# Holding back three of four gather groups on GpSimd until VectorE has made scores 0, 2 and the logits

## The reference

```python
# layer 0: deformable attention over 9 sampled points per pixel, 8 groups of 32 channels
qkv = depthwise3x3(groupnorm(x) @ qkv_w + qkv_b)
for g in range(8):
    off  = pconv_einsum(q, off_pconv_w[g], off_w[g]) + base[g]          # 9 (x, y) per pixel
    k, v = warp(k_map[g], off) * mask, warp(v_map[g], off) * mask       # bilinear, 4 corners
attn = softmax(q . k)                                                   # over the 9 points
x = x + (attn . v) @ proj_w + proj_b
# layer 1: attention of 8 heads over all 4096 tokens of an image, with 3-tap convolutions
t = layernorm(x); q, k, v = conv3(t), conv3(t), conv3(t)
t = x + t + conv3(softmax(q k^T / sqrt(32)) v)
# then a mixture of 8 experts (256 -> 1024 -> 256), each token sent to its best one
t = t + moe(layernorm(t))
```

## Time and profile before

| what | value |
|---|---|
| median of the runs | 12329.67 us |
| the profiled execution, its span | 12255.1 us |
| mean granted TensorE clock | 0.81 of 2.4 GHz |
| TensorE matmuls busy | 8279.2 us, 68% |
| VectorE busy | 5175.9 us, 42% |
| ScalarE busy | 3780.5 us, 31% |
| GpSimd busy | 4967.5 us, 41% |
| gathers of the sampling, L661 | 4608, of 1022 ns each on average |

### The profile page before, as it was taken

The page is one execution under the profiler, slowest core; times in us unless marked ns, Lnnn a source line. Parts: engine busy times, 40 slices in busy tenths (PEclk is TensorE's granted clock), DMA queues, the critical chain, the costliest instruction groups (busy, mean ns, idle before and its releaser), DMA issues. The chain is left out here.

```text
span 12255.1 us, 95913 instructions
## 1 busy us (share of the span) xinstructions
PE 8279.2 (68%) x31522; PEld 4334.5 (35%) x31522; DVE 5175.9 (42%) x10029; ACT 3780.5 (31%) x5495; POOL 4967.5 (41%) x4864
## 2 busy tenths in 40 slices
PE   6544656445663576666667765666666888998699
PEld 3522323332332233332333332333333333443366
DVE  6522334344443454444434443444444435663333
ACT  2100003001441144332434442324324563553122
POOL 1255564555445454454445554544554200000222
PEclk9776877666886688886878887778878898999799
DMA  3833233555332433333332334333343212113321
GB/s 133 281 93 89 92 124 111 185 194 158 95 91 86 128 99 97 93 100 107 94 97 89 103 91 121 110 114 99 98 123 95 70 45 74 41 45 80 123 71 49
DMA packets 658541, 1283.55 MB, mean 105 GB/s; under 512 B 189043, under 2 KB 398218, under 8 KB 643408
## 3 DMA queue, kind: packets, MB, share of 16 engines
q0 software_dynamic: 234240, 639.57, 17.4%
q1 hardware_dynamic: 405392, 562.58, 15.4%
q10 hardware_dynamic: 18432, 75.51, 1.5%
HBM read 1003.44 MB, written 278.91 MB: 105 GB/s over the span
## 5 line engine op out<-in xcount | busy, mean ns | idle before, releaser
L661 POOL DMA_INDIRECT sa_slot<-s_table,sa_rec x4608 | 4710.2, 1022 | 4902.7 <-DVE sa_vals L759 2347.2
L1651 DVE CUSTOM_DVE_ANT_0 a_above<-a_late,a_above 128x512 f32<-128x512 f32 x1600 | 1103.8, 690 | 3209.4 <-remote 1358.3
L1592 ACT ACTIVATE a_above<-a_diff 128x512 f32<-128x512 f32 x1600 | 956.4, 598 | 3189.2 <-DMA s_kd<-p_diff_lo 1408.5
L1558 PE MATMUL a_ctx<-a_p,a_v 128*64 128x512 f32 x6400 | 1714.9, 660 | 95.3 <-issue 95.2
L1583 ACT ACTIVATE a_p<-a_s 128x1024 f32<-128x1024 f32 x1600 | 1628.7, 1020 | 322.4 <-remote 163.3
L1503 PE MATMUL a_late<-a_k,a_q 96*128 96x512 f32 x1600 | 859.6, 537 | 838.5 <-DVE a_pair_max L1651 446.0
L1491 PE MATMUL a_diff<-a_kd,a_q 96*128 96x512 f32 x1600 | 773.9, 484 | 848.1 <-issue 460.6
L1541 PE MATMUL a_s<-a_q,a_k 98*128 98x512 f32 x3200 | 1110.2, 432 | 43.8 <-ACT a_p L1583 35.6
L816 PE MATMUL sa_sums<-keep_ident,sa_vals 128*128 128x128 f32 x4608 | 741.2, 308 | 565.8 <-issue 360.4
L1503 PEld LDWEIGHTS a_late<-a_k,a_q 96*128 96x128 f32 x1600 | 330.7, 207 | 1810.8 <-issue 1206.9
L816 PEld LDWEIGHTS sa_sums<-keep_ident,sa_vals 128*128 128x128 f32 x4608 | 640.4, 161 | 693.2 <-issue 445.6
(11 more groups left out here) (280 smaller groups left out, 8224.9 us busy)
## 6 DMA issues: line engine op xcount, KB each, us to landing
sa_slot<-s_table,sa_rec POOLq DMA_INDIRECT x4608
s_table<-t_rows ACTq DMA_DIRECT2D x64, 1024.0 KB, 7.5
a_q<-s_q SPq DMA_DIRECT2D x480, 128.0 KB, 2.6
s_part<-a_o SPq DMA_DIRECT2D x160, 256.0 KB
t_qwin<-s_dwq SPq DMA_DIRECT2D x64, 512.0 KB
t_kvwin<-s_dwkv SPq DMA_DIRECT2D x64, 386.0 KB
a_kd<-s_kd SPq DMA_DIRECT2D x384, 64.0 KB
a_o<-s_part SPq DMA_DIRECT2D x96, 256.0 KB, 2.7
```

The costliest lines, as they stand in the source:

```text
L661: pool.indirect_dma_start(out=self.slot[g][:, k, :, :, :].rearrange("p c a n -> p (c a n)"), out_offset=None, in_=self.s["table"][n // TIL ...
L1558: mm = pe.matmul(self.ps_ctx[i * 2 * HD:(i + 1) * 2 * HD, :], self.v_and_ones(run.head, kb), self.p[slot % P_SLOTS][:, i * CHUNK:(i + 1) * ...
L1592: act.activation(self.above[slot % n][:, :], self.ps_diff, ACT.Relu).then_inc(self.diff_got, 1)
L1651: dve.tensor_tensor_reduce(above, self.ps_late, above, 1.0, LOWEST, ALU.add, ALU.max, self.pair_max[:, t, j:j + 1]).then_inc(self.late_got, 1)
```

## The change

GpSimd waits more. A group's gather still waits until its slot is free. Groups 1, 2, 3 (and 5, 6, 7) now also wait for `chain`, that is for VectorE's place in the half tile that follows the values which freed the slot: group 1 until the first scores of that half are made (its piece m = 1), group 2 until the third (m = 5), group 3 until three operations of the logits are made (m = 8). Group 0 (and 4) is gathered as soon as its slot is free, as before. The gathers of tile 0 have no wait.

```diff
         if n > 0:
             pool.wait_ge(self.values_made, G * (n - 1) + g + 1)
+            if g % 4:
+                pool.wait_ge(self.chain, self.held_for(n, g))
         for k in range(K):
             pool.indirect_dma_start(
...
+    LINKS = 2 + 2 * G + 2 * (3 + 4)
+
+    def held_for(self, n, g):
+        n, i = (n - 1, 1) if g < 4 else (n, 0)
+        return (0, self.scored(n, 4 * i), self.scored(n, 4 * i + 2), self.scored(n, 4 * i + 3) + 3)[g % 4]
+
+    def scored(self, n, g):
+        return self.LINKS * n + 2 + 2 * (g + 1) + (3 + 4) * (g // 4)
```

More of the change, by code:

```diff
@@ L688, in vector @@
                 self.links += t.n
+                if m % HALF < 8 and m % HALF % 2:
+                    assert self.links == self.scored(n, 4 * (m // HALF) + m % HALF // 2)
     def tile_start(self, dve, t, n):
```

## The result

The changed kernel took 11480.73 us (median of four runs, 11433.48 to 11502.06) beside 12341.88 us for the kernel before in the same session (four runs, 12311.74 to 12356.55). A session here is one stretch of time on one chip, in which the kernels of one comparison are run. The ratio is 0.9297, 95% interval 0.9272 to 0.9321: faster by 7.0%. The forecast was 11650 us, the range 11050 to 12100. The span of the profiled execution fell from 12255.1 us to 11431.7 us, by 823 us where 680 had been forecast, and the granted clock rose from 0.808 to 0.830.

The account below looks back on a forecast made before the run. TensorE's signals, late while GpSimd gathers without a break, were taken to bound attention; span 12255.1 us less 680 (610 + 105 - 35) is 11575, plus 74.6 for the median of runs: 11650 us, range 11050 to 12100.

Parts of the forecast that it names:

- What bounds the kernel: In attention with sampling, TensorE's signals arrive late while GpSimd gathers without a break, the more so the longer it has.
- Attention, -610 us: Attention stages with sampling: a half tile takes 64.5 us against 72.65, 11.2% of 5445 us; bounds -1580 and -330.
- Where the groups fall: Attention: pauses after groups 0 and 1; groups 2, 3 and the next 0 run as one 36 us burst, group 1 alone.
- The ages of the earlier trace: Attention steps by 12 us of burst age: 2.70, 3.35, 6.0, 13.6 us, outside bursts 2.63; the 64.5 us rests on them.
- rival 1: Bursts break up fully since stalls delay the releases: 51 to 57 us a half tile, 10800 to 11200 us; chance 0.20.
- Projections and tables, -105 us: Projections and image 1's tables hold such stalls too; a third of attention's share, 4%: -105 us, between 0 and -300.
- Maps and stage ends, +35 us: First maps stage gains nothing; held groups left over at the ends of maps and tables cost +35 us, up to +50.
- Work that is now later: Group 3, released 44 us before its product, keeps 27 us in hand; VectorE's gather waits (286.3 us) grow by under 100.
- The clock: Sign in the profile after: mean granted clock above 0.81, toward 0.86.
- Short pauses clear nothing: Rival in attention: pauses of a microsecond leave one endless burst, 68 us a half tile or above, 12000 us; chance 0.14.
- It is not the length of a burst: Rival: lateness goes with the number of gathers, still 36, or something else late in a half; 12330 us, chance 0.06.
- Stage ends: Rival: at stage or block ends VectorE waits 26 us for held groups, 730 us in all; 12730 us, chance 0.10.

## Why the prediction was right, and where it was not

**What bounds the kernel.** TensorE's late signals while GpSimd gathers: right where the forecast was measured. Held gathers took time out of just the "remote" waits (1358 to 889 to 554 us), and a third of the DMAs, spaced, left none. *The more so the longer it has gathered* is the part that is not shown (see the burst of 43 gathers). The prediction did not ask whether the stalls belong to the kernel or to the occasion; nothing in one trace could have told it.

**Attention, -610 us.** All sampling attentions took 64.2 us a half tile, and 609 us less for equal steps. The size came out right by luck. The 64.5 us were worked out for the ten half tiles alone, against 72.65, and these took 62.6, 13.9% less and not 11.2%; over all attentions it was 72.3 to 64.2, which is 11.2%. And two of its steps were wrong in opposite ways. *Where the groups fall* said bursts of 9 and 27; they are mostly 9 and 18, since the stall delays VectorE and with it the release, as the text itself had noted and set aside. That should have given less time. *The ages of the earlier trace rows*, by which the first 12 us of a burst cost nothing, did not carry over: the first 12 us take 2.96 us a step and not 2.70, the second 12 us of bursts that long 5.25 and not 3.35, and the rest some 3.2 and not 2.63. The ages were measured behind pauses of 14 to 38 us (the ten before the bursts of the earlier trace rows), when every burst was 36 gathers long. In the changed kernel the pauses are mostly under 5 us, and where a burst ends depends on the stalls. With the true pattern those ages give some 19 x 2.8 = 53 us (an estimate from the earlier trace rows), rival 1's value, almost 10 us less than the 62.6 measured in this stretch.

**Projections and tables, -105 us.** Mis-sized: they measured -169 (122 + 47). The run with holds outside attention shows why a share per stage was the wrong form of estimate: only some 72 us of them (57 + 15) are there with their own holds alone, the rest only with the attention before them held.

**Maps and stage ends, +35 us.** Not seen: the maps came out 47 us shorter, not longer, and L723's waits did not grow, so nobody waited for groups left over at a stage's end. Why the maps were shorter is open, since the run with holds outside attention did not repeat it.

**Work that is now later.** Right: VectorE's waits for gathers are 286.4 us against 286.3, under the 100 us of growth allowed. A rule of the Trainium skill (DMA: Bandwidth & Descriptors, rules for kernel authors) would have DMAs issued early. Here issuing 27 of 36 later won 7.0%. With late signals absent it changed nothing, 0.9998. In neither case did the rule's gain show: with late signals the lead was longer than needed, and without them GpSimd hardly ever had to stop for a hold (139 us).

**The clock.** 0.808 to 0.830, below the 0.86 named; the stretch of ten half tiles rose from 0.84 to 0.89.

**The rivals.** *The bursts break up fully* (1): the release did follow the stall, but a broken burst is not a free one; the changed kernel's groups of nine took 2.96 us a step, and two or three released at a time still left 58 to 61 us a half tile. *Short pauses clear nothing* (2) fell, though half of it is true: some 3.2 us a step outside the bursts says that short pauses clear only part. *It is not the length of a burst* (3) fell as a forecast where signals are late: the number of gathers stayed 36 a half tile, and something was won. But its doubt about the length stands, and fewer DMAs did remove the lateness. In the other sessions its number came out, 0.9998, for another reason: there was nothing to win. The rule beside it, by which TensorE waits on no one (the Trainium skill, SBUF - State Buffer, two separate sides), speaks of memory ports. The run with half the bytes agrees that traffic is not it. What waits here are TensorE's partners, for its signals, 17.9 us in the earlier trace rows, and TensorE then waits for them, 15.00 us. The Trainium skill (DMA: Bandwidth & Descriptors, why a DMA increments its semaphore by 16) says that a DMA issued by GpSimd has all 16 engines post their own update whatever its shape. That would fit a cost by DMA and not by byte, as measured at 0.9994, and by it the 512 B rows change nothing. But the number of rows and GpSimd's time for a gather were the same too, so it is not shown. *Stage ends* (4) fell with the unchanged wait at L723.

## What to carry to other kernels

Read a long wait twice: when did the producer end, and when did the waiter start. If the signal and not the work is late, look at what another engine issues meanwhile, and spread its many small DMAs over the consumer's progress by waits on a counter that exists anyway. Here finer pieces won more (10.3% with two or three gathers, 7.0% with nine). Do not read a law out of stretches that the stall itself has sorted: bursts of 18 and of 36 looked quite different at the same age. And run the kernel before in several sessions before a gain is believed: this one is 7.0% in one and 0.0% in another, each with a tight interval.

## What the runs showed of the hardware

- One program, unchanged, took 12.3 ms in four sessions and 9.67 ms in three, with at most 0.6% between its runs in a session and no session in between. In the first kind TensorE's completion signals came late during long series of indirect DMAs, by 17.9 us in the example of the earlier trace rows.
- In the kernel before the steps of attention slowed with the age of a burst (2.70 us a step, then 3.35, 6.0, 13.6). That is no fixed law: one burst of 43 gathers ran at 2.4 us a step for 36 us. With short pauses the steps are slower from the start (2.96 us) and outside the bursts too (some 3.2 us).
- It goes with the indirect DMAs, not with their bytes: 9 per group, 12.3 ms with rows of 1 KB or 512 B alike (48 or 32 packets each); 3 per group, in threes 8.6 us apart, 9.77 ms, with GpSimd busy for 90% of the stretch.
- The granted clock follows the stalls: 0.84 where a half tile took 72.65 us, 0.89 at 62.6 us, 1.00 at 49.4 us.
- An indirect DMA of 128 rows takes GpSimd the same time with half the bytes: 378.10 / 361 = 1.05 us, against 374.46 / 360 = 1.04 us.
